# A graph-attention layer in fp32: where the turns of the probabilities and the second pair's scores stand between the projections

## The reference

```python
h = maximum(layernorm(x), 0)
q, k, v = h @ wq.T + bq, h @ wk.T + bk, h @ wv.T + bv
q2 = (q @ wiq.T + biq).reshape(N, H, D).transpose(1, 0, 2)      # the same for k2, v2
scores = einsum('hnd,hmd->hnm', q2, k2) / 8 + mask[None]
attn = softmax(scores, axis=-1)
out = einsum('hnm,hmd->hnd', attn, v2).transpose(1, 0, 2).reshape(N, 1024)
x + out @ wo.T + bo
```

## Time and profile before

| what | value |
|---|---|
| median of three runs | 291.98 us (291.90 to 292.07) |
| the profiled execution | 291.85 us, of which 290.1 us are the span of the trace |
| PE busy | 284.4 us, 98% of the span |
| DVE, ACT, POOL busy | 178.0, 159.8 and 152.9 us |
| one pass of the loop over pairs | 13.4 us |

### The profile page before, as it was taken

One profiled execution on the slowest core, in us unless ns is written; L12 is line 12 of the kernel. 1 busy time (PEld: TensorE's weight loads), 2 busy tenths in 40 slices (PEclk: granted clock), 3 DMA queues, 4 the chain that ended last, 5 costly groups with the idle time before them and its releaser, 6 DMA issues.

```text
span 290.1 us, 5957 instructions
## 1 busy us (share of the span) xinstructions
PE 284.4 (98%) x2325; PEld 265.6 (92%) x2325; DVE 178.0 (61%) x442; ACT 159.8 (55%) x287; POOL 152.9 (53%) x157
## 2 busy tenths in 40 slices
PE   6999999999999999999999999999999999999996
PEld 3799998888899999999999999999999999787885
DVE  4999878787587444433494866666666657743121
ACT  2886444182265443342244778787888788875000
POOL 6452455635355665545103796675949494696000
PEclk9999999999999999999999999999999999999999
DMA  7878965644843433356884251523223140230032
GB/s 260 319 245 278 326 208 170 235 139 158 348 145 104 158 111 87 124 145 147 240 189 114 60 132 36 128 66 83 73 75 105 44 146 2 76 134 10 2 145 72
DMA packets 16078, 40.90 MB, mean 141 GB/s; under 512 B 3737, under 2 KB 5170, under 8 KB 16050
## 3 DMA queue, kind: packets, MB, share of 16 engines
q1 hardware_dynamic: 13602, 38.53, 41.5%
q0 software_dynamic: 2016, 1.21, 1.9%
q10 hardware_dynamic: 432, 0.79, 0.7%
HBM read 37.71 MB, written 2.81 MB: 140 GB/s over the span
## 4 chain that ended last, share of the span: by engine, by line
PE 94%; DMA 2%; DVE 1%; ACT 1%; SPq 0%; issue 0%; ACTq 0%
PE banks L1105 23%; PE banks L978 19%; PE banks L980 19%; PE banks L979 19%; PE banks L1162 6%; PE banks L1124 5%; PE banks L1146 3%; DMA x_sb<-in_x 2%; PE banks L1027 1%; PE banks L1067 1%; PE banks L1057 0%; PE banks L1070 0%; ACT x_sb L586 0%; ACT prob L650 0%; SPq L359 0%
## 5 line engine op out<-in xcount | busy, mean ns | idle before, releaser
L484 POOL DMA_INDIRECT cells<-value,cell x51 | 54.6, 1070 | 54.8 <-DMA cells<-value,cell 41.5
L538 ACT ACTIVATE w_hi<-raw 128x1024 fp32r<-128x1024 f32 x50 | 51.7, 1055 | 22.7 <-PE banks L980 19.1
L978 PE MATMUL banks<-a_hi,w_hi 128*128 128x384 f32 x184 | 61.5, 334 | 0.0
L980 PE MATMUL banks<-a_lo,w_hi 128*128 128x384 f32 x184 | 61.5, 334 | 0.0
L979 PE MATMUL banks<-a_hi,w_lo 128*128 128x384 f32 x184 | 61.5, 334 | 0.0
L457 POOL TENSOR_TENSOR w_lo<-raw,w_hi 128x1024 fp32r<-128x1024 f32 x15 | 36.7, 2448 | 39.8 <-ACT w_hi L538 39.8
L838 DVE TENSOR_TENSOR w_lo<-raw,w_hi 128x1024 fp32r<-128x1024 f32 x35 | 42.3, 1229 | 9.9 <-ACT w_hi L538 9.9
L978 PEld LDWEIGHTS banks<-a_hi,w_hi 128*128 128x128 f32 x184 | 34.5, 188 | 0.1
L979 PEld LDWEIGHTS banks<-a_hi,w_lo 128*128 128x128 f32 x184 | 34.5, 188 | 0.0
L980 PEld LDWEIGHTS banks<-a_lo,w_hi 128*128 128x128 f32 x184 | 34.5, 188 | 0.0
L650 ACT ACTIVATE prob<-prob,neg_max 128x384 f32<-128x384 f32 x48 | 29.1, 607 | 8.5 <-DVE neg_max L898 8.3
(11 more groups left out here) (146 smaller groups left out, 597.6 us busy)
## 6 DMA issues: line engine op xcount, KB each, us to landing
raw<-in_slabs SPq DMA_DIRECT2D x40, 512.0 KB, 3.6
raw<-in_slabs SPq DMA_DIRECT2D x32, 256.0 KB, 4.1
prob<-key_rows SPq DMA_DIRECT2D x8, 256.0 KB, 4.4
x_sb<-in_x SPq DMA_DIRECT2D x3, 512.0 KB, 5.4
out_y<-x_sb SPq DMA_DIRECT2D x5, 256.0 KB, 2.1
cells<-prob SPq DMA_DIRECT2D x2, 576.0 KB, 7.8
cells<-value,cell POOLq DMA_INDIRECT x51, 4.0
x_sb<-in_x ACTq DMA_DIRECT2D x3, 256.0 KB, 4.2
```

Of the source, the lines that this page charges most:

```text
L484: nc.gpsimd.indirect_dma_start(out=cells[c][:, :], out_offset=bass.IndirectOffsetOnAxis(ap=cell[:, t:t + 1], axis=0), in_=value[:, t:t + 1 ...
L538: nc.scalar.activation(split_place(s)[0], raw_place(s), ACT.Copy).then_inc(slab_hi, 1)
L978: nc.tensor.matmul(psum, w[0], a[0], start=first, stop=False)
L980: return nc.tensor.matmul(psum, w[0], a[1], start=False, stop=last)
```

## The change

Two sets of numbers in PE's instruction list are changed. Pair 2 gets 15 steps, not 12, ahead of the first scores of pair 1, and correspondingly 3, not 6, behind them. In each of the six passes, turn 1 stands 4 steps behind turn 0 (before: 6), turn 2 again 4 steps behind turn 1, and 8 steps (before: 6) stand between turn 2 and the values. No instruction is added or taken away, and the lists of DVE, ACT, POOL and SyncE (SP) stay as they are.

```diff
-            pair_steps(2, 0, 12)
+            pair_steps(2, 0, 15)
             for j in range(1, PAIRS - 1):
                 scores(j, 0)
-                pair_steps(j + 1, 12 if j == 1 else 8, 18 if j == 1 else 16)
+                pair_steps(j + 1, 15 if j == 1 else 8, 18 if j == 1 else 16)
...
                 turn(j - 1, 0)
-                pair_steps(j + 1, 32, 38)
+                pair_steps(j + 1, 32, 36)
                 turn(j - 1, 1)
-                pair_steps(j + 1, 38, 42)
+                pair_steps(j + 1, 36, 40)
                 turn(j - 1, 2)
-                pair_steps(j + 1, 42, 48)
+                pair_steps(j + 1, 40, 48)
                 pair_values(j - 1)
```

## The result

The changed kernel takes 293.10 us, median of seven runs (292.87 to 294.47), against 291.98 us, median of seven runs (291.81 to 292.08). The ratio is 1.0048, with a 95% interval of 1.0032 to 1.0063: slower, by 1.1 us. The profiled execution took 293.1 us, of which 291.4 us are the span.

What follows compares the result with a forecast made beforehand. The prediction took TensorE, busy 98% of the span, as the bound, so only its idle moments count. Its terms, -0.44 + 2.04 - 0.36 = +1.24 us, gave a median of 293.2 us, range 292.3 to 294.1.

Steps and rivals of the forecast that it cites:

- Place A: Pair 1's first scores, once: PE waits for DVE's `k_lo`; three more steps ahead cover it, -0.44 us.
- Place B: Turn 2, six times: it waits for `pt_lo` of turn 0, so moving it nearer stalls PE 0.34 us each, +2.04 us.
- part 1: Three more steps ahead of pair 1's first scores: -0.44 us there, with effects behind them costed at nothing.
- Place C: Behind a pair's values, six times: PE waits for `k_lo`; eight steps after turn 2 bring it 0.06 us earlier, -0.36 us.
- The clock: Rival, in the passes: PE's clock falls to half pace, over 296 us for even a third of one pass; chance 0.02.

Runs made afterwards that it cites:

- first part alone: Against the kernel before, only pair 2's steps ahead of pair 1's first scores went from 12 to 15, turns untouched: 291.44 us, ratio 0.9984.
- second part alone: Against the kernel before, only the turns' spacing was changed, to 8, 4, 4, 8, with 12 steps kept ahead of pair 1's first scores: 293.40 us, ratio 1.0048.
- the first four experiments: Against the kernel before: only 15 steps at the scores; only the turns moved; turn 1 early; the new spacing in other banks: 291.44, 293.40, 291.52, 290.93 us.
- the kernel with six steps: Against the kernel before: 15 steps at the scores, turns at 8, 4, 2, 10, so six steps between turn 0 and turn 2: 295.12 us, ratio 1.0105.

## Why the prediction was right, point by point

- **Place A**, forecast -0.44 us: -0.46 us by the run with the first part alone. The start moved by the three steps, and the sequence in the trace has no gap. The load comes just in time, as forecast, at its full lead and 0.06 us behind the end of `k_lo`.
- **Place B**, forecast +2.04 us: 0.41 + 5 x 0.32 = 2.01 us by the trace. The four passes that aren't worked out here are like the one that is: in all five turn 2 starts 2.51 us behind turn 0. The load starts 0.05 us behind the end of `pt_lo` on both sides of the change. That the wait is the whole loss is shown by the run in other banks; that turn 1 has no part in it, by the run with turn 1 early and turn 2 where it was.
- **How the stall is made up** was different, and that the sums agree so closely is in part luck. The prediction let the transposes start 0.07 us behind their load; a held turn starts together with it (within 0.01 us), so that the gap is 0.26 us, the prediction's lower end, and not 0.34. What it didn't count is the 0.06 us lost inside the turn. The two misses, -0.08 and +0.06 us in each pass, nearly cancel. The first pass is 0.08 us longer still, since ACT doesn't come forward with PE; the prediction had put everything that part 1 does behind place A at nothing.
- **Place C**, forecast -0.36 us: about 6 x 0.08 = 0.48 us by the trace. Behind the start of the values the second double comes after 2.37 to 2.41 us in the six passes before, and after 2.30 to 2.31 us in the six of the changed kernel; the mean difference is 0.08 us. `q_lo` starts 0.03 us behind `q_hi`, as forecast. The size was 0.02 us per pass too small. That `pt_lo` of turn 2 is what held it is shown by the run with turn 2 later.
- **The sum**, forecast +1.24 us and 293.2 us: measured +1.12 us and 293.1 us. A pass was forecast at about 13.7 us; it takes 13.63 to 13.64 us.
- **The clock** did not fall in six pauses of a third of a microsecond, one in each pass of 13.6 us: the granted clock is 1.00 in every window shown, and in the top tenth in all forty slices. What the Trainium skill says in "TensorE: Matmul & The Clock Gate", section "A second HAM failure mode: psum-queue depth-cycling", of small pauses between groups of matmuls that cycle through PSUM banks, gives no effect here. The pauses of this kernel are simply paid once.
- Of the profiled difference, 293.1 - 291.85 = 1.25 us, 0.26 us, about a fifth, is no effect of the change: pair 0's first scores start that much later in the profiled execution of the changed kernel, ahead of all that was changed. Timeline of PE, before, then after:

```profile
156.56 0.34 PE L1124 MATMUL banks<-k_hi,q_hi 64*128 64x384 f32 x2
```

```profile
156.82 0.35 PE L1124 MATMUL banks<-k_hi,q_hi 64*128 64x384 f32 x2
```

That start differs between any two executions: over the nine kernels profiled it lies between 156.35 and 156.83 us, though all of them have the same instructions up to there. The view of PE's waits differs there too; for line 1027, where PE waits for ACT's `x_sb`, it lists up to 1.5 us in some and nothing in others. (Before the change it lists 0.2 us, which the earlier trace rows and the prediction leave out.)

Open is why the seven runs of the changed kernel spread over 1.6 us and the seven of the kernel before over 0.3 us. The stalls by themselves don't explain it: the kernel with the second part alone has them too and spreads over 0.3 us, and the kernel before, timed 21 times beside the first four experiments, spread over 1.3 us (291.69 to 292.98).

## What to carry to other kernels

When an engine seems never to wait, compare its starts with its own pace, and the start of each load with that of its matmul: a load that always starts the same few hundredths of a microsecond behind another engine's end is a wait without slack, though no view of the kernel before listed it. Moving two pieces of work closer together pays only until the second meets the buffer of the first; from there every step moved costs its full time, in this kernel 0.17 us in each of six passes. A buffer taken from elsewhere (here the banks of the values, for which turn 1 did not have to wait) can remove such a wall, and only then did the new spacing bring a gain.

## What the runs showed of the hardware that was not expected

A stalled turn costs more than its gap. After a wait its first transpose and its load start together (214.91 and 214.92 in the kernel with six steps), and the step behind comes 0.39 us later in place of 0.33 to 0.34. That is 0.06 us per stall, as the distance to the values also shows, about half of the 0.11 us that the scores' doubles lost at their restart in the earlier trace rows.
